# Gated graph network layer with tiles in groups of four, first states joined as 16-bit planes in two pieces, and the work on finished tiles spread out

## What is computed

```python
h = jnp.maximum(_layernorm(x, axis=-1), 0.0)
for l in range(5):
    m   = jnp.einsum('bnd,de->bne', h, weight[l])
    agg = jnp.einsum('bij,bid->bjd', A, m)          # A = (adj != 0)
    gi, gh = agg @ w_ih.T + b_ih, h @ w_hh.T + b_hh
    r = sigmoid(i_r + h_r);  z = sigmoid(i_z + h_z);  n = tanh(i_n + r * h_n)
    h = (1.0 - z) * n + z * h
return x + h * mask[..., None]
```

## Time and profile before

| | |
|---|---|
| time, 3 runs | median 377.11 us (376.7 to 378.42) |
| the profiled execution | 377.65 us, of which the span on the core is 375.9 us |
| granted TensorE clock | 0.996 of full over the span |
| busy share | PE 97%, DVE 83%, ACT 79%, POOL 73% |
| DMA | 44.46 MB, mean 118 GB/s |
| POOL `zh` (L778) | 80 times, 1272 ns each |
| POOL `hp` low half (L783) | 64 times, 1156 ns each |
| POOL mask product (L790) and sum (L794) | 14 and 15 times, 1305 and 1272 ns |
| DVE join (L648) | 6 times, 1499 ns on average |
| PE fp32 transposes (L356) | 40 of 128 columns, four to a tile |

### The profile page before, as it was taken

One profiled execution on the slowest core, in us unless ns is written; L12 is line 12 of the kernel. 1 busy time (PEld: TensorE's weight loads), 2 busy tenths in 40 slices (PEclk: granted clock), 3 DMA queues, 4 the chain that ended last, 5 costly groups with the idle time before them and its releaser, 6 DMA issues.

```text
span 375.9 us, 6545 instructions
## 1 busy us (share of the span) xinstructions
PE 363.5 (97%) x2152; PEld 184.0 (49%) x2152; DVE 310.2 (83%) x572; ACT 297.6 (79%) x495; POOL 275.7 (73%) x258
## 2 busy tenths in 40 slices
PE   7899999999999999999999999999999999999992
PEld 3454555555555544445444545544455545555441
DVE  4879888888878788798989898888878787777775
ACT  5988898998878888798888887687677776677662
POOL 3759779788778979587695876867877655555796
PEclk9999999999999999999999999999999999999998
DMA  8536535747744556745364774327734423287422
GB/s 259 189 58 140 114 74 123 175 95 180 169 111 111 86 94 121 150 87 114 83 115 112 146 192 82 88 58 161 134 70 102 97 56 58 56 228 184 95 84 84
DMA packets 102176, 44.46 MB, mean 118 GB/s; under 512 B 91392, under 2 KB 91776, under 8 KB 102144
## 3 DMA queue, kind: packets, MB, share of 16 engines
q1 hardware_dynamic: 102000, 43.80, 51.7%
q10 hardware_dynamic: 144, 0.26, 0.2%
HBM read 17.57 MB, written 4.19 MB: 58 GB/s over the span
## 4 chain that ended last, share of the span: by engine, by line
PE 79%; DVE 9%; POOL 5%; DMA 2%; issue 2%; SPq 1%; ACT 1%; DVEq 0%; POOLq 0%
PE ps_r L273 8%; PE ps_z L275 8%; PE ps_z L274 8%; PE ps_z L273 8%; PE ps_r L275 8%; PE ps_r L274 8%; PE ps_s L347 4%; PE ps_s L346 4%; PE ps_in L275 4%; PE ps_in L274 4%; PE ps_in L273 4%; PE ps_hn L273 4%; PE ps_hn L275 4%; PE ps_hn L274 4%; DVE ps_in L605 1%
## 5 line engine op out<-in xcount | busy, mean ns | idle before, releaser
L778 POOL TENSOR_TENSOR zh<-z,h 128x512 f32<-128x512 f32 x80 | 101.8, 1272 | 77.3 <-ACT z L461 77.0
L455 ACT ACTIVATE r<-ps_r,b_sum,unscale 128x512 f32<-128x512 f32 x80 | 62.2, 778 | 46.9 <-PE ps_r L275 46.0
L465 ACT ACTIVATE ps_in<-ps_in,b_ih,unscale 128x512 f32<-128x512 f32 x80 | 60.0, 751 | 19.2 <-DVE ps_in L605 17.5
L783 POOL TENSOR_TENSOR hp<-h,hp 128x512 f16<-128x512 f32 x64 | 74.0, 1156 | 1.3 <-ACT hp L471 1.3
L599 DVE SCALAR_TENSOR_TENSOR rhn<-ps_hn,b_hn,r 128x512 f32<-128x512 f32 x80 | 59.9, 749 | 17.1 <-ACT r L455 16.8
L605 DVE TENSOR_TENSOR ps_in<-ps_in,rhn 128x512 f32<-128x512 f32 x80 | 56.0, 699 | 16.0 <-PE ps_in L275 13.7
L611 DVE SCALAR_TENSOR_TENSOR ps_in<-z,ps_in 128x512 f32<-128x512 f32 x79 | 54.6, 691 | 11.0 <-ACT ps_in L465 11.0
L461 ACT ACTIVATE z<-ps_z,b_sum,unscale 128x512 f32<-128x512 f32 x80 | 61.6, 770 | 0.7 <-PE ps_z L275 0.7
L616 DVE TENSOR_TENSOR h<-zh,ps_in 128x512 f32<-128x512 f32 x78 | 53.6, 687 | 10.3 <-POOL zh L778 2.1
L593 DVE TENSOR_TENSOR s_lo<-ps_s,s_hi 128x512 f16<-128x512 f32 x80 | 54.4, 680 | 0.4 <-ACT s_hi L449 0.4
L449 ACT CAST s_hi<-ps_s 128x512 f16<-128x512 f32 x80 | 46.6, 582 | 0.5
(11 more groups left out here) (109 smaller groups left out, 741.3 us busy)
## 6 DMA issues: line engine op xcount, KB each, us to landing
x_in<-in_x SPq DMA_DIRECT2D x16, 256.0 KB, 3.7
adj_in<-in_adj SPq DMA_DIRECT2D x16, 256.0 KB, 3.9
x_out<-in_xT SPq DMA_DIRECT2D x16, 256.0 KB, 3.1
mask_in<-in_mask_row SPq DMA_DIRECT2D x16, 256.0 KB, 3.6
out<-x_out SPq DMA_DIRECT2D x15, 256.0 KB, 2.3
nat<-hp SPq DMA_TRANSPOSE x64, 3.1
fold_in<-in_fold_lhs SPq DMA_DIRECT2D x1, 320.0 KB, 3.9
out<-x_out ACTq DMA_DIRECT2D x1, 256.0 KB, 2.6
```

The lines of the kernel that those rows point to most:

```text
L455: nc.scalar.activation(r[:], ps_r[:], ACT.Sigmoid, bias=b_sum[:, 0:1], scale=unscale[:, 0:1]).then_inc(r_done, 1)
L465: nc.scalar.activation(ps_in[K % 2][:], ps_in[K % 2][:], ACT.Tanh, bias=b_ih[:, 2:3], scale=unscale[:, 0:1]).then_inc(n_done, 1)
L778: nc.gpsimd.tensor_tensor(zh[:, K % 2], z[:, K % 2], h[:, t % RING], ALU.mult).then_inc(zh_done, 1)
L783: nc.gpsimd.tensor_tensor(h_lo(t), h[:, t % RING], h_hi(t), ALU.subtract).then_inc(h_lo_done, 1)
```

## The change

1. `GROUPS = (4, 4, 4, 4)`: four tiles in every group, so that every layer of a tile follows four units behind the last. `prep`, `ends` and all that hangs on them move.
2. `HALVES` is gone: every tile from 4 on takes the 16-bit planes, none of them the fp32 transpose on PE and ACT's copy from PSUM.
3. The join becomes two DVE copies of 512 halves, in stages 8 and 9 (`STAGES = 10`); the second sets `h_init`.
4. `ends` are spaced by `SPREAD = 5`, at a fixed distance from the preparation stages as long as there are any, and the sum of a tile is moved one slot behind its mask product (`adding`), with the store behind it (`storing`).
5. The mask products of tiles 12 and 13 move from POOL to DVE as well: units 76 to 78 leave their state in PSUM and DVE multiplies it right behind (`END`). `FINISH` goes from 5 to 3.
6. The fold of layer 1 moves on PE from the end of slot 2 to the point ahead of the first `s_product` of unit 0. ACT's and DVE's parts of it stay in slot 2.

With 5-slot spacing the side work of one tile and the end of another fall so (slot modulo 5): 3 loads, moments and natural halves; 4 moments' aggregation, inverse deviation, split; 0 adjacency; 1 first layer norm half, first join half, mask product; 2 second layer norm half, second join half, sum. `prep` is 4, 7, 10, 13 for tiles 4 to 7 (before: 1, 4, 7, 10) and 18, 23, ... 53 for tiles 8 to 15.

```diff
-GROUPS = (4, 6, 6)
+GROUPS = (4, 4, 4, 4)
-HALVES = 10
-FINISH = 5
-STAGES = 9
+FINISH = 3
+STAGES = 10
+SPREAD = 5
...
-        ends[t] = soon if t >= starts[-1] or not t else max(soon, ends[t - 1] + 3)
+        if t >= starts[-1]:
+            ends[t] = soon
+        elif t and ends[t - 1] > prep[TILES - 1]:
+            ends[t] = max(soon, ends[t - 1] + 3)
+        else:
+            ends[t] = max(soon, ends[t - 1] + SPREAD if t else 0)
+            ends[t] += (prep[TILES - 1] + 3 - ends[t]) % SPREAD
...
+    adds = {t: ends[t] + (ends[t] + 1 not in ending and ends[t] + 2 < N) for t in ends}
+    adding = {adds[t]: t for t in ends if t < TILES - 2}
+    storing = {adds[t] + 1: t for t in ends}
...
+                if K == 0:
+                    fold(1)
                 pe.wait_ge(s_lo_done, K + 1)
...
-                if tile_at_stage[5].get(K, HALVES) < HALVES:
-                    transpose_first(tile_at_stage[5][K])
...
-                if folding(K):
+                if folding(K) > 1:
                     fold(folding(K))
...
-                if K in tile_at_stage[6] and tile_at_stage[6][K] < HALVES:
-                    transposed(tile_at_stage[6][K])
-                if K in tile_at_stage[6] and tile_at_stage[6][K] >= HALVES:
+                if K in tile_at_stage[6]:
                     split(tile_at_stage[6][K])
...
-                out_ap = h[:, t % RING] if K < N - 2 else ps_in[K % 2][:]
+                out_ap = h[:, t % RING] if K < END else ps_in[K % 2][:]
...
-                if tile_at_stage[8].get(K, 0) >= HALVES:
-                    join(tile_at_stage[8][K])
+                for half in range(2):
+                    if K in tile_at_stage[8 + half]:
+                        join(tile_at_stage[8 + half][K], half)
...
-                if K == N - 2:
+                if END <= K < N - 1:
                     masked_state(K)
...
-                if K in ending and K < N - 1:
-                    final(ending[K])
+                if K in ending and ending[K] < starts[-1]:
+                    masked_result(ending[K])
+                if K in adding:
+                    final(adding[K])
```

More of the change, by code:

```diff
@@ L47, in gnn_kernel @@
     at = {u: K for K, u in enumerate(units)}
+    END = at[starts[-1], LAST]
     inner = [sum(l < LAST for _, l in units[:K + 1]) for K in range(N)]
@@ L54, in gnn_kernel @@
     for t in reversed(range(FIRST, TILES)):
-        gap = 3 if t < starts[1] + GROUPS[1] else 5
+        gap = 3 if t < starts[1] + GROUPS[1] else SPREAD
         prep[t] = min(at[t, 0] - STAGES, prep[t + 1] - gap if t + 1 < TILES else N)
@@ L59, in gnn_kernel @@
         soon = at[t, LAST] + 1
-        ends[t] = soon if t >= starts[-1] or not t else max(soon, ends[t - 1] + 3)
+        if t >= starts[-1]:
[5 more added lines that the diff above has]
+            ends[t] += (prep[TILES - 1] + 3 - ends[t]) % SPREAD
     tile_at_stage = [{prep[t] + s: t for t in prep} for s in range(STAGES)]
     ending = {ends[t]: t for t in ends}
+    adds = {t: ends[t] + (ends[t] + 1 not in ending and ends[t] + 2 < N) for t in ends}
+    adding = {adds[t]: t for t in ends if t < TILES - 2}
+    storing = {adds[t] + 1: t for t in ends}
     fetching = {ends[t] - FETCH: [t] for t in ends}
-    fetching[N - FINISH - FETCH].append(TILES - 1)
+    fetching.setdefault(N - FINISH - FETCH, []).append(TILES - 1)
     xT_t = xT.rearrange("d (t c) -> t d c", c=TILE)
@@ L157, in gnn_kernel @@
         nat_hi_init, nat_lo_init = sem("nat_hi_init"), sem("nat_lo_init")
-        split_done = sem("split_done")
+        split_done, half_joined = sem("split_done"), sem("half_joined")
         h_hi_init, h_lo_init, h_init = sem("h_hi_init"), sem("h_lo_init"), sem("h_init")
@@ L211, in transpose_halves @@
             def transpose_halves(t):
-                sp.wait_ge(split_done, t - HALVES + 1)
-                if t - HALVES >= 2:
+                sp.wait_ge(split_done, t - FIRST + 1)
+                if t - FIRST >= 2:
                     sp.wait_ge(h_init, t - 1)
@@ L260, in _ @@
                     transpose_first(tile_at_stage[6][K])
[L261 to L264, removed]
+                    transpose_halves(tile_at_stage[6][K])
+                if K in storing:
+                    store(storing[K])
                 for t in fetching.get(K, ()):
@@ L414, in layernorm @@
                     act.wait_ge(nat_lo_init, t - LN + 1)
-                    act.wait_ge(t_mm, min(t - LN + 1, HALVES))
+                    act.wait_ge(t_mm, min(t - LN + 1, FIRST))
                 for q in (2 * half, 2 * half + 1):
@@ L434, in transposed @@
                     act.wait_ge(h_lo_init, t + 1)
-                if t >= RING:
-                    act.wait_ge(masked, t - RING + 1)
                 nc.scalar.activation(h[:, t % RING], ps_t[:], ACT.Relu).then_inc(h_init, 1)
@@ L441, in split @@
                 act.wait_ge(h0_done, 2 * t + 2)
-                if t - HALVES >= 2:
-                    act.wait_ge(halves_loaded[t % 2], 16 * ((t - HALVES) // 2))
+                if t - FIRST >= 2:
+                    act.wait_ge(halves_loaded[t % 2], 16 * ((t - FIRST) // 2))
                 nc.scalar.copy(halves[:, t % 2], h0[:, t % LN].bitcast(U16).rearrange("p (c b) -> p b c", b=2)).then_inc(
@@ L642, in last_result, with join @@
                 nc.vector.tensor_tensor(x_out[:, f], x_out[:, f], ps_in[K % 2][:], ALU.subtract).then_inc(last_out, 1)
-            def join(t):
-                dve.wait_ge(halves_loaded[t % 2], 16 * ((t - HALVES) // 2 + 1))
+            def join(t, half):
+                dve.wait_ge(halves_loaded[t % 2], 16 * ((t - FIRST) // 2 + 1))
                 if t >= RING:
                     dve.wait_ge(masked, t - RING + 1)
-                nc.vector.tensor_copy(h[:, t % RING].bitcast(U16).rearrange("p (c b) -> p b c", b=2),
-                               halves_t[:, t % 2].rearrange("p (b g) c -> p b (g c)", b=2)).then_inc(h_init, 1)
+                two = slice(2 * half, 2 * half + 2)
+                state = h[:, t % RING].rearrange("p (g c) -> p g c", g=TG)[:, two].rearrange("p g c -> p (g c)")
+                joined = nc.vector.tensor_copy(state.bitcast(U16).rearrange("p (c b) -> p b c", b=2),
+                                               halves_t[:, t % 2].rearrange("p (b g) c -> p b g c", b=2)[:, :, two].rearrange(
+                                                   "p b g c -> p b (g c)"))
+                joined.then_inc(h_init if half else half_joined, 1)
             def v_low(l):
@@ L783, in state_low, with masked_result @@
                 nc.gpsimd.tensor_tensor(h_lo(t), h[:, t % RING], h_hi(t), ALU.subtract).then_inc(h_lo_done, 1)
+            def masked_result(t):
+                f = t % FRING
+                pool.wait_ge(ends_loaded[f], 32 * (t // FRING + 1))
+                pool.wait_ge(h_done, at[t, LAST] + 1)
+                nc.gpsimd.tensor_tensor(mask_in[:, f], mask_in[:, f], h[:, t % RING], ALU.mult).then_inc(masked, 1)
             def final(t):
                 f = t % FRING
[L787 to L790, removed]
+                if t < starts[-1]:
                     pool.wait_ge(masked, t + 1)
                 else:
-                    pool.wait_ge(last_masked, 1)
+                    pool.wait_ge(last_masked, t - starts[-1] + 1)
                 nc.gpsimd.tensor_tensor(x_out[:, f], x_out[:, f], mask_in[:, f], ALU.add).then_inc(out_done, 1)
```

## The result

| | before | after |
|---|---|---|
| time, median of 6 runs | 377.1 us (376.64 to 378.42) | 373.5 us (373.11 to 373.83) |
| ratio | | 0.9899, 95% interval 0.9881 to 0.9917 |
| profiled execution, span | 377.65, 375.9 us | 373.38, 371.5 us |

The forecast was 372.0 us in a range from 370.3 to 375.0. The change makes the kernel 3.6 us faster, 1.0%; 5.1 us were expected.

What follows compares the result with a forecast made beforehand. PE, busy 97% of the span, was taken as the bound, with a floor of 4.33 us a slot. Gains of 6.4 less costs of 1.25 net 5.1, so 377.11 becomes 372.0 us, range 370.3 to 375.0.

Steps and rivals of the forecast that it cites:

- PE transposes, 2.64: PE, tiles 4 to 9: six fp32 transposes of 0.44 us each go, all on the path, gaining 2.64 us.
- Stalls in slots 23 to 57, 3.4 taken as gone: Slots 23 to 57: POOL bursts, late planes, joins and last preparations cost 3.4 us, which the new spacing removes.
- (a): POOL doing adjacency, mask product and sum in one slot makes zh late; PE's next s-product comes at 134.52, not 133.86.
- Half joins, 0.33 behind POOL and no stall: DVE's half joins end 0.33 us behind POOL's low half, 0.28 earlier than whole ones; 24 of them cost zero.
- Rival 1: Half joins on DVE cost as much as whole ones, 0.2 us each, giving 376 us; chance 0.08.
- rival 3: The join loses its place to POOL's queued instruction, PE starts about 1.0 us late, time up to near 388; chance 0.04.
- Slots 9 to 19, 0.8 taken: Tiles three slots apart: costs of 0.15 us from ACT, 0.25 from POOL, 0.4 from late state transposes.
- Groups of four, cost 0: State transposes have 2.0 us in hand for all units, over 10 in groups of six; cost taken as 0.
- Rival 2: State transposes land at 5.6 us instead of 3.1 in groups of four, slots 20 to 59: 376 us; chance 0.05.
- The fold, 0; slot 3, 0.39: Moving the fold gains 0, as slot 2 waits for tile 3's transpose; slot 3 gains 0.39 us from later tile 4 work.
- Rival 4: The fold's move gains its 0.65 us if tile 3's transpose lands earlier, giving 371.4 us; chance 0.05.
- The tail, 0.25 lost and POOL's relief worth nothing: Units 77 to 79: DVE's added mask product delays PE, cost 0.25 us; relieving POOL gains nothing, since DVE ends the chain.

Runs made afterwards that it cites:

- the spreading run: The changed kernel with POOL's sum back in the slot of the mask product, right behind it; 375.26 us, ratio 0.9926.
- the repeat: The changed kernel measured again without any edit; 373.68 us, ratio 0.9894.

## Why the prediction was right, point by point

- **What bounds the kernel:** right. 4.33 us a slot is the floor in every kernel, and every gain and loss could be read as a slot above it. The excess was 11.0, not 10.9 (79 slots are 342.2), and what stands beside transposes and folds in the first four and the last slot is 1.1, not 0.9.
- **PE transposes, 2.64:** right; the slots 6, 9, 12, 15, 18 and 21 lose 0.44 each. Their price on the other engines is the term below.
- **Stalls in slots 23 to 57, 3.4 taken as gone:** right, 3.33 to 0.27, and what is left has another cause. The burst on POOL (a) made zh and h late as the text says, but about half of slot 25 was DVE's pause, which the prediction did not see; that it went too was luck, as it goes by the place in DVE's program. POOL's second way to PE, through the low half and the state transposes, was only found by the spreading run.
- **Half joins, 0.33 behind POOL and no stall:** right, 0.32 and none in 18 slots; whole joins cost 0.2 each. The Trainium skill's formula for a DVE copy from SBUF ("VectorE: DVE Perf Modes", the TRN2 errata) gives an estimate of 0.33 for the half; the trace agrees with 0.32 behind POOL's end, but the one half join that began with POOL idle (slot 19) took 0.44. Rival 1 is refuted, and rival 3 too: POOL's queued instruction gave way in slots 21 to 61. The 0.2 for slots 37 and 57 did not come (0.00).
- **Slots 9 to 19, 0.8 taken:** the place was right, the size was not: 1.29. 0.28 of it, slot 13, is DVE's pause, which the sum did not have. Slots 14 and 15 lose 0.42 to a late s_lo. There DVE has no idle time: its second half join waits for POOL, which is late by its pair of adjacency and natural low half, and DVE's part of a fold comes on top. For POOL and ACT 0.40 was taken; ACT, with 0.15 of it, has no part, as s_lo waits for DVE's own instructions. Slots 16 and 17 lose 0.59 to a late state transpose and a late s_lo; 0.4 was taken. The upper bound of the range was added up wrong as well: the bounds of these three terms are 3.5 over what was taken, not 3, which makes 375.5.
- **Groups of four, cost 0:** right for the changed kernel, but with less in hand than the text says. One piece more on POOL was enough to use it up. Rival 2, landings of 5.6, did not come: the longest of the 64 is 4.5 in the changed kernel.
- **The fold, 0; slot 3, 0.39:** both right. Rival 4 is refuted.
- **The tail, 0.25 lost and POOL's relief worth nothing:** both halves were wrong and nearly cancel. DVE is late twice in a row and the lateness adds up, 0.48 in slot 78: 1.66 behind the slot's start in a plain slot, r_times_hn starts at 1.98 in slot 77 and at 2.23 in slot 78. Timeline of DVE in these two, and PE behind them:

```profile
355.81 0.74 DVE L606 SCALAR_TENSOR_TENSOR rhn<-ps_hn,b_hn,r 128x512 f32<-128x512 f32 x1
...
360.39 0.74 DVE L606 SCALAR_TENSOR_TENSOR rhn<-ps_hn,b_hn,r 128x512 f32<-128x512 f32 x1
...
362.58 0.39 PE L284 MATMUL ps_z<-s_hi,v_hi 128*128 128x512 f16 x1 [0.53 <-DVE s_lo L600]
```

  Against it stand 0.53 at the end. The step that failed is "POOL's relief there is worth nothing, since DVE ends the chain". DVE's last sum and the store of tile 15 did end the chain, and in both kernels that sum starts 4.8 behind the start of unit 79. But in the kernel before POOL was so late that the store of tile 14 was issued 0.08 ahead of the last one. Timelines of SP and ACT, before:

```profile
372.55 0.33 SPq L232 DMA_DIRECT2D out<-x_out  x1
372.63 0.37 ACTq L487 DMA_DIRECT2D out<-x_out  x1
```

  The last store then took 2.6 us to land; in the changed kernel it is issued 0.6 behind tile 14's and takes 2.1. The last column of the page's rows, before and after:

```profile
out<-x_out ACTq DMA_DIRECT2D x1, 256.0 KB, 2.6
```
```profile
out<-x_out ACTq DMA_DIRECT2D x1, 256.0 KB, 2.1
```

- **The sum.** Gains 2.64 + 3.3 + 0.39 = 6.3, as forecast within 0.1. Costs 1.29 + 0.48 + 0.27 + 0.44 (the later start of slot 1, not shown to be the change's) - 0.53 = 1.95 instead of 1.25; 6.3 - 1.95 = 4.4, the difference of the spans (375.9 - 371.5). By the medians of the times it is 3.6, since the execution of before lay 0.5 above its median, as the prediction says, and the changed one 0.1 below. Beside the repeat, on another chip, it is 4.0 (377.66 to 373.68). The forecast was 1.5 too low, half by these terms and half by the execution that the rows came from.

## What to carry to other kernels

When one engine is always busy, take the starts of its periodic instruction, subtract the pace of a clean stretch, and account for every period that is longer; terms of 0.2 us in 370 can then be forecast and checked. Count the room of a chain over all its links: a late instruction may have room for its own reader and none for the one behind it in the same queue. And size a piece of side work by what remains in hand after it, since a copy cut in two can cost nothing where the whole one costs 0.2 us each time. Look for short pauses of an engine behind its own instructions before a late chain is put down to another engine.

## What the runs showed of the hardware

- A DVE copy of 16-bit halves nearly always waited for POOL's running instruction and then held POOL off: the 24 half joins of the changed kernel lasted 0.44 to 1.29 us. Beside a running POOL instruction they ended 0.31 to 0.32 behind it, and where one stood queued on POOL they came ahead of it. One whole join in the kernel before with planes did not wait: it ran from 91.27 to 92.02, 0.75 long, in the midst of POOL's adjacency (90.37 to 92.48).
- DVE stood still for 0.45 to 0.48 us between two dependent instructions of its own, at the same two instructions in all executions with the same DVE program (and at two others in the kernel before), and not in slot 52 when 40 empty waits came before. Cause open.
- The same sixteen blank products took 4.94 to 6.59 us in different executions. Slot 1 began anywhere from 18.91 to 19.95, and not in the order of these times.
- State transposes landed in 3.1 us in the median and in up to 4.9 (6.0 in the kernel with groups of 4, 6 and 6), the longest beside loads and stores.
- A store of 256 KB landed in 2.6 us when another was issued 0.08 ahead of it, and in 2.1 when that was 0.6 ahead.
